# First FFN layer as seven block products with a running sum in PSUM, its operands streamed like the last layer's, and the h2 sums, the residual and the weight sums on GpSimd

## The chip, the cores and the metric

One core of one Trainium2 chip runs the whole program. The metric is the device time of one execution in microseconds (us); lower is better.

## What is computed

Cut to what matters (16 graphs of 1024 nodes, 256 features, 8 experts; everything in fp32):

```python
x = x + gnn(layernorm(x), adj, W, a)              # attention over the graph, per graph 1024 x 1024
n = layernorm(x)                                  # from here on: the FFN layer
w = softmax(mean(n, axis=0) @ Wr + br)            # 8 gates per node
h = relu(bn1(einsum('bfd,edh->bfeh', n, W1) + b1))    # first layer, 8 experts
h = relu(bn2(einsum('bfeh,ehk->bfek', h, W2) + b2))   # second layer
y = einsum('bfeh,ehd->bfed', h, Wo) + bo              # last layer
x = x + einsum('bfed,fe->bfd', y, w)
```

## The kernel before, in words

`attention_block` goes through the 16 graphs in 8 pairs of 16 row tiles (128 rows each) and writes x1, the input of the FFN, to HBM. Beside it each pair loads two matrices of W1 and W2 and splits them into an upper and a lower fp32r part (ACT L742, POOL L539); they stay in SBUF. Its last slots also start the FFN: normalisation of tile 0, the first gates, the first matmuls of step 0.

`ffn_block` works on 32 tiles of 512 rows (kept transposed: 2 blocks of 128 features by 512 rows) and, for each, on 8 experts: 256 steps. Every product is made in three matmuls (upper x upper, upper x lower, lower x upper), so each operand is first split: ACT copies it to fp32r (the upper part), DVE subtracts that from the original (the lower part). One step is:

- first layer (`z_layer(0, ...)`, L53 to L55): 2 x 2 blocks, 12 matmuls of 512 columns, into two PSUM banks; ACT applies batch norm and relu (L1331), splits (L1361), DVE makes the lower part (L1446);
- second layer (`z_layer(1, ...)`): again 12 matmuls of 512 columns; ACT batch norm and relu (L1331);
- DVE multiplies by the gate (L1488) and makes the block sums T1, T3 (L1495), T2 (L1498), T4 (L1501) of the seven-product scheme (Strassen's, in Winograd's form); ACT splits 7 blocks of 256 columns at once (L1347), DVE makes their lower part (L1481);
- last layer (`y_layer`, L1199 to L1202): seven block products, 21 matmuls of 256 columns, summed over the 8 experts in PSUM. Its weight sums are made in the first 8 steps by DVE and ACT (`LastWeights`), stored to HBM, and from step 8 on 896 KB of operands are loaded per step (L1105), beside 256 KB of gate rows (L1082).

The order of the work is written out by hand. Each engine runs `slot(u)` for u = -4 to 255 in its own instruction order; slot u holds the last layer of step u, the second layer of step u+2 and the first layer of step u+4. Engines meet only through semaphores, and each runs its list strictly in order. Work that comes once per tile (8 slots) is put into named slots: transposes of x (L1172) and y (L1180) on PE, copies of the seven sums out of PSUM (ACT L1386, DVE L1510), their combination (L1430), the lower part of x (L1409), the residual (L1422) and layer-norm statistics (L74, L81) on DVE, normalisation (L1315) on ACT. GpSimd has only five operations of 4 columns per tile (L87 to L90, L1148 to L1155).

Of the kernel before, what the change touches and what calls it, by code (L numbers as in the profile page):

```python
# [23 lines left out]
ALU = mybir.AluOpType  # L24
# [33 lines left out]
class TileNorm:  # L58
# [3 lines left out]
    def __init__(self, keep, sem, minus_half, ln_eps, CT, D):  # L62
        self.CT, self.minus_half, self.ln_eps = CT, minus_half, ln_eps
        self.xn = keep("ffn_xn", [P, CT, D])
        self.stats, self.mv = keep("ffn_stats", [P, CT, 6]), keep("ffn_mv", [P, CT, 2])
        self.vareps, self.rstd = keep("ffn_vareps", [P, CT]), keep("ffn_rstd", [P, CT])
        self.stat, self.mv_ready, self.vareps_ready = sem("ffn_stat"), sem("ffn_mv_ready"), sem("ffn_vareps_ready")
        self.rstd_ready, self.xn_ready = sem("ffn_rstd_ready"), sem("ffn_xn_ready")

    def statistics(self, dve, x1, x1_in, turn, rows=None):  # L70

        dve.wait_ge(x1_in, DMA * turn)
        for s in range(self.CT) if rows is None else rows:
            dve.bn_stats(self.stats[:, s, :], x1[:, s, :]).then_inc(self.stat, 1)  # L74

    def mean_var(self, dve, n, waited):

        if not waited:
            dve.wait_ge(self.stat, self.CT * n)
        for s in range(self.CT):  # L80
            last = dve.bn_aggr(self.mv[:, s, :], self.stats[:, s, :])  # L81
        last.then_inc(self.mv_ready, 1)

    def deviation(self, pool, n):

        pool.wait_ge(self.mv_ready, n)
        pool.tensor_tensor(self.vareps[:, :], self.mv[:, :, 1], self.ln_eps[:, :], ALU.add) \  # L87
            .then_inc(self.vareps_ready, 1)
        pool.wait_ge(self.vareps_ready, n)
        pool.tensor_tensor(self.rstd[:, :], self.vareps[:, :], self.minus_half[:, :], ALU.pow) \  # L90
            .then_inc(self.rstd_ready, 1)

    def normalise(self, dve, x1, n):

        dve.wait_ge(self.rstd_ready, n)
        for s in range(self.CT):
            last = dve.tensor_scalar(self.xn[:, s, :], x1[:, s, :], self.mv[:, s, 0:1], self.rstd[:, s:s + 1],
                                     ALU.subtract, ALU.mult)
        last.then_inc(self.xn_ready, 1)


class FirstTile:
# [15 lines left out]
class LastWeights:
# [5 lines left out]
    def __init__(self, sem, shared, Wo):  # L124
        self.Wo, self.E, self.KB = Wo, Wo.shape[0], Wo.shape[1] // P
        self.ops = [shared.wh_lo[:, 0:7, :].rearrange("p q (h c) -> p (q h) c", h=2)
                    .rearrange("p (i q) c -> p i q c", i=2), None]
        self.sums = [shared.x_rows[:, i * 4:(i + 1) * 4, :].rearrange("p s (h d) -> p (s h) d", d=P) for i in range(2)]
        self.loaded = [sem(f"wo_sums_in{i}") for i in range(4)]
        self.sum_ready, self.hi_ready, self.lo_ready = sem("wo_sum_ready"), sem("wo_hi_ready"), sem("wo_lo_ready")  # L130

    def home(self, e):

        return (0, 0) if e == 0 else ((1, 2, 3)[(e - 1) % 3], (e - 1) // 3)

    def load(self, sp, e):
        i, _ = self.home(e)
        for m in range(self.KB):
            sp.dma_start(self.sums[i][:, (1 - m):4:2, :],
                         self.Wo[e].rearrange("(k p) d -> p k d", p=P)[:, :, m * P:(m + 1) * P]) \  # L140
                .then_inc(self.loaded[i], DMA)

    def add_blocks(self, dve, e):

        i, turn = self.home(e)
        s, done = self.sums[i], 4 * e
        dve.wait_ge(self.loaded[i], DMA * self.KB * (turn + 1))
# [86 lines left out]
def program(nc, x, adj, W, a, Wr, br, W1, b1, g1, be1, m1, v1, W2, b2, g2, be2, m2, v2, Wo, bo, out):  # L234
# [1341 lines left out]
```

## Time and profile before

| | |
|---|---|
| median of 3 runs | 2841.0 us (2841.0 to 2842.17) |
| the profiled execution, its own time | 2841.68 us |
| its span, first to last instruction | 2839.8 us |
| busy: PE, PE weight loads, DVE, ACT, POOL | 2779.0, 2472.5, 2403.8, 2116.8, 487.6 us |
| attention, then FFN (first FFN instruction) | about 708.7 us, then 2131 us |
| DMA moved | 445.91 MB, mean 157 GB/s |

Matmul records overlap (each lasts longer than the distance to the next), so the distance between starts is what one costs PE. "idle before" is the engine's idle time ahead of an instruction with what ended it; "issue" there means that nothing the profile shows was waited for. Times in timelines are us from the start of the span.

### The profile page before, as it was taken

How to read it: one execution, taken by the hardware profiler on the slowest of the kernel's cores; microseconds unless marked ns; L12 is line 12 of the kernel's file. 1: busy time of each engine (PE TensorE's matmuls, PEld its weight loads, DVE VectorE, ACT ScalarE, POOL GpSimd, SP SyncE). 2: the span in 40 equal slices, each digit the busy share in tenths (PEclk: the TensorE clock that was granted, in tenths of full speed). 3: DMA queues.
4: the chain of work that ended last, by engine and by line, in shares of the span. 5: the costliest groups of instructions: out<-in, count | busy, mean ns of one | idle time of the engine just before them, and what ended most of it. 6: DMA issues, size and time to landing. Idle time of an engine off the chain costs nothing.

```text
span 2839.8 us, 46078 instructions
## 1 busy us (share of the span) xinstructions
PE 2779.0 (98%) x17110; PEld 2472.5 (87%) x17110; DVE 2403.8 (85%) x3376; ACT 2116.8 (75%) x2847; POOL 487.6 (17%) x704
## 2 busy tenths in 40 slices
PE   7999999998899999999999999999999999999998
PEld 7999999998788888888888888888888888888887
DVE  7999999997788888888888888888888888888887
ACT  6888888887677777767777767777777777777775
POOL 3555555455000000000000001000000000000000
PEclk9999999999999999999999999999999999999999
DMA  4555455443454554555545544555555555545454
GB/s 146 162 159 161 151 163 160 153 158 98 132 170 151 170 158 157 167 158 161 165 153 161 164 153 162 159 164 164 153 168 165 153 162 165 155 159 165 151 163 141
DMA packets 160060, 445.91 MB, mean 157 GB/s; under 512 B 16032, under 2 KB 73800, under 8 KB 159840
## 3 DMA queue, kind: packets, MB, share of 16 engines
q1 hardware_dynamic: 159840, 442.98, 49.7%
q8 instruction: 138, 2.26, 0.3%
q14 instruction: 82, 0.67, 0.1%
HBM read 401.99 MB, written 40.93 MB: 156 GB/s over the span
## 4 chain that ended last, share of the span: by engine, by line
PE 73%; DVE 1%; ACT 0%; issue 0%; DMA 0%; POOL 0%; DVEq 0%; ACTq 0%; POOLq 0%
PE head_ps L53 12%; PE head_ps L55 12%; PE head_ps L54 12%; PE m_ps L1199 7%; PE m_ps L1201 7%; PE m_ps L1202 7%; PE z_ps L53 4%; PE z_ps L55 4%; PE z_ps L54 4%; PE turn_ps L1172 1%; PE turn_ps L1180 1%; ACT h L1331 0%; DVE h_sums L1488 0%; DVE h_lo L1446 0%; DMA wo_ops<-wo_scratch 0%
## 5 line engine op out<-in xcount | busy, mean ns | idle before, releaser
L1331 ACT ACTIVATE h<-head_ps,bn_shift,bn_scale 128x512 f32<-128x512 f32 x768 | 593.7, 773 | 538.8 <-PE head_ps L55 331.7
L1481 DVE TENSOR_TENSOR h_lo<-h_sums,h_hi 128x1792 fp32r<-128x1792 f32 (+1 forms) x257 | 518.3, 2017 | 198.9 <-ACT h_hi L1347 198.8
L1347 ACT ACTIVATE h_hi<-h_sums 128x1792 fp32r<-128x1792 f32 (+1 forms) x257 | 435.5, 1694 | 63.3 <-DVE h_sums L1501 57.9
L1488 DVE TENSOR_TENSOR h_sums<-h,gate_row 128x1024 f32<-128x1024 f32 x256 | 313.8, 1226 | 121.0 <-ACT h L1331 103.7
L87 POOL TENSOR_TENSOR ffn_vareps<-ffn_mv,ln_eps 128x4 f32<-128x4 f32 x32 | 7.9, 248 | 1865.7 <-DVE ffn_mv L81 1865.7
L1446 DVE TENSOR_TENSOR h_lo<-h,h_hi 128x1024 fp32r<-128x1024 f32 x256 | 312.0, 1219 | 6.9 <-ACT h_hi L1361 6.9
L53 PE MATMUL attn_ps<-wh_hi,pT_hi 128*128 128x256 f32 x1024 | 305.1, 298 | 0.0
L54 PE MATMUL attn_ps<-wh_lo,pT_hi 128*128 128x256 f32 x1024 | 288.4, 282 | 0.0
L55 PE MATMUL attn_ps<-wh_hi,pT_lo 128*128 128x256 f32 x1024 | 288.4, 282 | 0.0
L1361 ACT ACTIVATE h_hi<-h 128x1024 fp32r<-128x1024 f32 x256 | 270.8, 1058 | 0.1
L1199 PE MATMUL m_ps<-h_hi,wo_ops 128*128 128x256 f32 x896 | 256.6, 286 | 3.0 <-DMA wo_ops<-wo_scratch 3.0
L1199 PE MATMUL m_ps<-h_hi,wh_lo 128*128 128x256 f32 x896 | 256.3, 286 | 0.0
L1201 PE MATMUL m_ps<-h_lo,wo_ops 128*128 128x256 f32 x896 | 250.8, 280 | 0.0
L1201 PE MATMUL m_ps<-h_lo,wh_lo 128*128 128x256 f32 x896 | 250.4, 279 | 0.0
L1202 PE MATMUL m_ps<-h_hi,wo_ops 128*128 128x256 f32 x896 | 250.3, 279 | 0.0
L1202 PE MATMUL m_ps<-h_hi,wh_lo 128*128 128x256 f32 x896 | 250.1, 279 | 0.0
L53 PE MATMUL head_ps<-wh_hi,w_hi 128*128 128x512 f32 x512 | 204.4, 399 | 7.4 <-ACT h L1331 7.4
L55 PE MATMUL head_ps<-wh_hi,w_lo 128*128 128x512 f32 x512 | 203.2, 397 | 0.0
L54 PE MATMUL head_ps<-wh_hi,w_hi 128*128 128x512 f32 x512 | 203.2, 397 | 0.0
L53 PE MATMUL head_ps<-xT_hi,w_hi 128*128 128x512 f32 x512 | 202.7, 396 | 0.0
L55 PE MATMUL head_ps<-h_hi,w_lo 128*128 128x512 f32 x512 | 201.3, 393 | 0.0
L53 PE MATMUL z_ps<-h_hi,w_hi 128*128 128x512 f32 x512 | 200.7, 392 | 0.5 <-DVE h_lo L1446 0.4
(198 smaller groups left out, 7619.1 us busy)
## 6 DMA issues: line engine op xcount, KB each, us to landing
wh_lo<-wo_scratch SPq DMA_DIRECT2D x124, 896.0 KB, 6.3
wo_ops<-wo_scratch SPq DMA_DIRECT2D x124, 896.0 KB, 6.5
adj_sb<-in_adj SPq DMA_DIRECT2D x128, 512.0 KB, 3.5
gate_row<-w_scratch SPq DMA_DIRECT2D x256, 256.0 KB, 4.6
x_sb<-in_x SPq DMA_DIRECT2D x64, 256.0 KB, 2.9
x_scratch<-x_sb SPq DMA_DIRECT2D x128, 128.0 KB, 1.9
ffn_x<-x_scratch SPq DMA_DIRECT2D x16, 512.0 KB, 7.6
x_sb<-x_scratch SPq DMA_DIRECT2D x16, 512.0 KB, 7.7
```

The source lines that it names most:

```text
L53: pe.matmul(out, w_hi, x_hi, start=first, stop=False)
L54: pe.matmul(out, w_hi, x_lo, start=False, stop=False)
L55: return pe.matmul(out, w_lo, x_hi, start=False, stop=last)
L1199: pe.matmul(m_at(q), w_hi, x_hi[:, x, :], start=e == 0 and q in OPENERS, stop=False, skip_group_check=True)
L1201: pe.matmul(m_at(q), w_hi, x_lo[:, x, :], start=False, stop=False, skip_group_check=True)
L1202: done = pe.matmul(m_at(q), w_lo, x_hi[:, x, :], start=False, stop=e == E - 1, skip_group_check=True)
L1331: return act.activation(dst, src, ACT.Relu, bias=bn_shift[layer][:, col], scale=bn_scale[layer][:, col])
L1347: act.activation(h2_hi[s % 2][:, a:b, :], g2[:, 1 + a:1 + b, :], ACT.Copy) \
L1361: act.activation(h1_hi[s % 2][:, :, :], h1[:, :, :], ACT.Copy).then_inc(S["h1_hi_ready"], 1)
L1446: dve.tensor_tensor(h1_lo[s % 2][:, :, :], h1[:, :, :], bits(h1_hi[s % 2][:, :, :]), ALU.subtract) \
L1481: dve.tensor_tensor(h2_lo[s % 2][:, a:b, :], g2[:, 1 + a:1 + b, :], bits(h2_hi[s % 2][:, a:b, :]), ALU.subtract).then_inc(S["h2_lo_ready"], 1)
L1488: dve.tensor_tensor(h2_rows, h2[:, :, :], gate[s % 2][:, :].unsqueeze(1).to_broadcast([P, KB, BANK]), ALU.mult).then_inc(S["gated_ready"], 1)
```

## The change

The first layer is made by seven block products too. The order of the work on PE in slot u (z = u+4, s2 = u+2) is now written as pieces between which ACT reads the running sum:

```diff
+            def extend_run(s, a, t, done):
+                pe.wait_ge(S["snap_ready"], 3 * s + done)
+                first_product(s, run, a, t, False, done == 3).then_inc(S["run_psum"], 1)
+            def corners(s):
+                wait(pe, S["c12_ready"], s)
+                first_product(s, Z_P2, A12, B21, True, True)
+                first_product(s, Z_P5, S1, T1, False, False).then_inc(S["c_psum"], 1)
...
             def slot(u):
+                second_layer(u + 2, 0)      # 6 matmuls of 512 columns
+                last_corner(z - 1)          # 3 of 256: S4 x B22
+                begin_run(z)                # 3: A11 x B11
...
+                last_layer(u, 0, 2)         # 6 of 256
+                second_layer(s2, 1)         # 6 of 512; waits relu2_ready
+                extend_run(z, S2, T2, 1)    # 3
+                corners(z)                  # 6
+                last_layer(u, 2, 4)         # 6
+                extend_run(z, S3, T3, 2)    # 3
+                last_layer(u, 4, 6)         # 6
+                extend_run(z, A22, T4, 3)   # 3
+                last_layer(u, 6, 7)         # 3
```

(The calls are written shorter than in the file; there each stands behind `is_step`.) ACT takes three snapshots of the running sum (256 columns, with the batch-norm shift) and the final value; the batch-norm scale is multiplied into W1 beforehand. DVE adds the corners, and its split now applies relu as well:

```diff
+            def snapshot(s, i):
+                act.wait_ge(S["run_psum"], 4 * s + (i + 1))
+                dst = (snaps[:, 0, :], h1_flat[:, 0:HALF], snaps[:, 1, :])[i]
+                act.activation(dst, run, ACT.Identity, bias=bn_shift[0][:, at:at + 1]).then_inc(S["snap_ready"], 1)
+            def first_sums(s):
+                dve.tensor_tensor(h1_flat[:, HALF:3 * HALF], snaps[...], bank_c, ALU.add)
+            def last_sum_first(s):
+                dve.tensor_tensor(h1_flat[:, 0:HALF], h1_flat[:, 0:HALF], Z_P5, ALU.add)
+            def first_lower(s, part):         # 256 and 768 columns, both operands in SBUF
+                dve.scalar_tensor_tensor(h1_lo, h1_flat, 0.0, bits(h1_hi), ALU.max, ALU.subtract)
```

Order in ACT's slot: `first_upper(z-1, 1)` (768 columns), `second_relu(s2, 0)`, `snapshot(z, 0)`, `first_upper(z-1, 0)` (256), `second_upper(s2-1, 1)` (1024), per-tile copies, `second_relu(s2, 1)`, `snapshot(z, 1)`, `blocks.upper(t, 1)` (1024, one slot in 8), `normalise`, `snapshot(z, 2)`, `second_upper(s2, 0)` (768), `c21(z)`, and in one slot in 8 the copy of the products. Order in DVE's slot: `second_lower(s2-1, 0)` (768), `first_lower(z-1, 1)` (768), `last_sum_first`, combinations, `blocks.lower` (768, 1024), `first_lower(z-1, 0)` (256), `second_lower(s2-1, 1)` (1024), `add_out`, `gated` (1024), `first_sums` (512), product copy.

The block sums of h2 move from DVE to GpSimd, with the residual and new block sums of x:

```diff
         def _(pool):
+            def residual(t, half):            # 512 columns, twice per tile
+                pool.tensor_tensor(rows, rows, w_bo[...], ALU.add)
+            def sums(s):                      # 512, 256, 256 columns
+                pool.wait_ge(S["gated_ready"], s + 1)
+                wait(pool, S["h2_lo1_ready"], s)
+                pool.tensor_tensor(g2[:, T1:T1 + 2, :], g2[:, B12, :]..., g2[:, B11:B11 + 2, :], ALU.subtract)
+                pool.tensor_tensor(g2[:, T2, :], g2[:, B22, :], g2[:, T1, :], ALU.subtract)
+                pool.tensor_tensor(g2[:, T4, :], g2[:, B21, :], g2[:, T2, :], ALU.subtract)
             def slot(u):
+                t = rows_due(u - 1, 1)        # u mod 8 == 2
+                if t is not None:
+                    blocks.sums(pool, t)      # 512, 256, 256 columns; waits for ACT's copies
+                for half in range(2):         # u mod 8 == 3 and 4
+                    residual(...)
+                sums(u + Z2)
```

The sums of W1 (scaled) and Wo, their split and their store move into the attention, on GpSimd (`OperandPrep`): per pair two scalings of 256 columns, eight sums of 128, two copies of 896 and two subtractions each of 384 and 512 columns; one of two weight splits (ACT L742, POOL L539) goes. In the FFN, SP loads 896 KB of W1 operands per step beside the 896 KB of Wo operands, the former after `c12_psum` of two steps before. Statistics of x1 are no longer made in the FFN: the mean and deviation that the attention computed are kept. The first matmuls of step 0 move from the attention's end into the FFN's first slot. The second layer's two halves now share one PSUM bank.

## Rows read from the trace of the kernel before

**Rows 1.** Engines' busy time over two stretches, attention and FFN.
```profile
core 0: us, PE busy (x) PEld busy (x) DVE busy (x) ACT busy (x) POOL busy (x), PEclk, DMA share, GB/s
100.00:700.00 600.00, 577.97 (x4476) 552.63 (x4475) 546.71 (x1016) 524.79 (x951) 329.97 (x474) 1.00 0.48 153
800.00:2800.00 2000.00, 1999.93 (x11442) 1743.13 (x11441) 1675.03 (x2030) 1437.52 (x1673) 104.93 (x145) 1.00 0.52 161
```
**Rows 2.** Timeline of PE: first matmul of three layers in one step (start, us).
```profile
2627.09 0.28 PE L1199 MATMUL m_ps<-h_hi,wo_ops 128*128 128x256 f32 x1
...
2629.54 0.39 PE L53 MATMUL head_ps<-xT_hi,w_hi 128*128 128x512 f32 x1
...
2632.29 0.39 PE L53 MATMUL z_ps<-h_hi,w_hi 128*128 128x512 f32 x1
```
**Rows 3.** Timeline of SP: the same issue one tile (8 steps) apart.
```profile
1529.83 0.32 SPq L1082 DMA_DIRECT2D gate_row<-w_scratch  x1
...
1595.59 0.32 SPq L1082 DMA_DIRECT2D gate_row<-w_scratch  x1
```
**Rows 4.** Groups of ACT and DVE, 1000 to 2700 us: busy, mean ns | idle before.
```profile
L1331 ACT ACTIVATE h<-head_ps,bn_shift,bn_scale 128x512 f32<-128x512 f32 x621 | 480.1, 773 | 432.8 <-PE head_ps L55 254.1 <-DVE h_lo L1446 178.6
L1481 DVE TENSOR_TENSOR h_lo<-h_sums,h_hi 128x1792 fp32r<-128x1792 f32 x208 | 421.1, 2025 | 164.0 <-ACT h_hi L1347 164.0
L1361 ACT ACTIVATE h_hi<-h 128x1024 fp32r<-128x1024 f32 x207 | 219.0, 1058 | 0.0
L1488 DVE TENSOR_TENSOR h_sums<-h,gate_row 128x1024 f32<-128x1024 f32 x207 | 253.7, 1226 | 94.4 <-ACT h L1331 80.2 <-DVE h_lo L1481 0.5
L1495 DVE TENSOR_TENSOR h_sums<-h_sums 128x512 f32<-128x512 f32 x207 | 141.7, 684 | 0.0
L1498 DVE TENSOR_TENSOR h_sums<-h_sums 128x256 f32<-128x256 f32 x207 | 88.0, 425 | 7.2
```
**Rows 5.** Groups of ACT in the attention: an evacuation of 256 columns with one column operand.
```profile
L728 ACT ACTIVATE wh_hi<-head_ps,xs_rstd 128x256 fp32r<-128x256 f32 x124 | 51.9, 470 | 2.4 <-PE head_ps L628 2.4
```
**Rows 6.** Timeline: PE to ACT, and PE starting again behind ACT.
```profile
1501.47 0.39 PE L55 MATMUL head_ps<-h_hi,w_lo 128*128 128x512 f32 x1
...
1501.91 0.78 ACT L1331 ACTIVATE h<-head_ps,bn_shift,bn_scale 128x512 f32<-128x512 f32 x1 [0.32 <-PE head_ps L55]
...
734.94 0.78 ACT L1331 ACTIVATE h<-head_ps,bn_shift,bn_scale 128x512 f32<-128x512 f32 x1
...
735.78 0.50 PE L53 MATMUL head_ps<-wh_hi,w_hi 128*128 128x512 f32 x1 [1.16 <-ACT h L1331]
...
736.12 0.40 PE L54 MATMUL head_ps<-wh_hi,w_hi 128*128 128x512 f32 x1
```
**Rows 7.** Groups of POOL, whole run.
```profile
L533 POOL TENSOR_TENSOR node_table<-node_table,n_sb 128x512 f32<-128x512 f32 x65 | 84.1, 1294 | 5.1
...
L522 POOL TENSOR_TENSOR xs_vareps<-xs_mv,ln_eps 128x2 f32<-128x2 f32 x64 | 12.5, 195 | 42.4 <-DVE xs_mv L857 42.4
```
**Rows 8.** Timelines of POOL and DVE in the attention, three meetings.
```profile
351.02 1.27 POOL L533 TENSOR_TENSOR node_table<-node_table,n_sb 128x512 f32<-128x512 f32 x1
352.26 1.10 POOL L562 TENSOR_SCALAR n_sb<-x_sb,x_negmean,x_rstd 128x256 f32<-128x256 f32 x2
...
352.94 1.50 DVE L905 SCALAR_TENSOR_TENSOR scores<-adj_sb,ej_rows 128x1024 f32<-128x1024 int32 x1 [1.07 <-issue]
...
329.66 1.20 DVE L905 SCALAR_TENSOR_TENSOR scores<-adj_sb,ej_rows 128x1024 f32<-128x1024 int32 x1
...
329.78 1.66 POOL L525 TENSOR_TENSOR xs_rstd<-xs_vareps,minus_half 128x2 f32<-128x2 f32 x1
...
332.51 0.69 POOL L525 TENSOR_TENSOR xs_rstd<-xs_vareps,minus_half 128x2 f32<-128x2 f32 x1
...
298.53 2.06 POOL L562 TENSOR_SCALAR n_sb<-x_sb,x_negmean,x_rstd 128x256 f32<-128x256 f32 x2
...
299.89 1.23 DVE L913 TENSOR_TENSOR pT_lo<-pT_ps,pT_hi 128x1024 fp32r<-128x1024 f32 x1 [0.26 <-ACT pT_hi L760]
```
**Rows 9.** Timeline of PE: the longest wait at the FFN's start.
```profile
748.72 0.80 PE L53 MATMUL head_ps<-wh_hi,w_hi 128*128 128x512 f32 x1 [4.66 <-ACT h L1331]
749.32 0.63 PE L54 MATMUL head_ps<-wh_hi,w_hi 128*128 128x512 f32 x1
749.75 0.63 PE L55 MATMUL head_ps<-wh_hi,w_lo 128*128 128x512 f32 x1
```
**Rows 10.** DMA issues, whole run: KB each, median us from issue to landing.
```profile
wo_ops<-wo_scratch SPq DMA_DIRECT2D x124, 896.0 KB, 6.5
...
gate_row<-w_scratch SPq DMA_DIRECT2D x256, 256.0 KB, 4.6
```

More of the change, by code:

```diff
@@ L84, in deviation @@
[L84 to L98, printed above, removed]
-        last.then_inc(self.xn_ready, 1)
+        self.negmean, self.rstd, self.shift = (keep(f"row_{n}", [P, tiles]) for n in ("negmean", "rstd", "shift"))
@@ L113, in __init__ @@
         self.wT = norm.xn[:, 0:2, :].rearrange("p s d -> p (s d)")
         self.wh_lo = keep("wh_lo0", [P, TB, D], FP32R)
+        self.wo_ops = self.wh_lo[:, 0:7, :].rearrange("p q (h c) -> p (q h) c", h=2).rearrange("p (i q) c -> p i q c", i=2)
+        self.w1_ops = keep("w1_ops0", [P, 2, 7, P], FP32R)
+        self.wo_in, self.w1_in = sem("wo_ops_in0"), sem("w1_ops_in0")
         self.x_rows = keep("x_sb0", [P, TB, D])
-class LastWeights:
+class OperandPrep:
     A21, A11, A22, A12, S1, S3, S2, S4 = range(8)
[L124 to L137, printed above, removed]
-        for m in range(self.KB):
[L139 to L147, printed above, removed]
@@ new lines, in scale_blocks, with sums @@
+    def scale_blocks(self, pool, e):
+        pool.wait_ge(self.blocks_in, 2 * DMA * (2 * e + 1))
+        pool.wait_ge(self.scale_in, DMA * (e + 1))
+        for m in range(self.KB):
+            part = self.blocks[:, (1 - m):4:2, :]
+            pool.tensor_tensor(part, part,
+                               self.scale[:, m * P:(m + 1) * P].unsqueeze(1).to_broadcast([P, self.KB, P]), ALU.mult) \
+                .then_inc(self.scaled, 1)
+    def sums(self, pool, n):
+        b, done = self.blocks, 4 * n
+        if n % 2 == 0:
+            pool.wait_ge(self.scaled, n + 2)
+        else:
+            pool.wait_ge(self.blocks_in, 2 * DMA * (n + 1))
@@ L495, in _ @@
             sp.wait_ge(small_in, DMA * 13)
+            sp.wait_ge(prep.stored, DMA * 2 * E)
         @block.gpsimd
@@ L804, in slot @@
                     for d in range(KB):
[L805 to L807 removed]
+                        blocks.copy(act, head_ps[:, d, :], 0, d, norm.root)
                 if last and u == GATE_SLOT + 1:
[L809 removed]
+                    for part in range(2):
+                        blocks.upper(act, 0, part)
                 if last and u == GATE_SLOT + 2:
@@ L1129, in _ @@
             load_x1(1)
-            for e in range(2, 4):
-                last_w.load(sp, e)
+            load_wo(1)
             for u in range(-Z1, NS):
@@ new lines, in first_product, with begin_run @@
+            def first_product(s, acc, a, t, first, stop):
+                i = (s // E) % 2
+                return product(acc, w1_ops[s % 2], blocks.hi[i], blocks.lo[i], a, t, first, stop)
+            def begin_run(s):
+                pe.wait_ge(w1_in[s % 2], DMA * (s // 2 + 1))
+                if s % E == 0:
+                    pe.wait_ge(blocks.lo_ready, 2 * (s // E + 1))
+                wait(pe, S["c21_ready"], s)
+                first_product(s, run, A11, B11, True, False).then_inc(S["run_psum"], 1)
```

765 lines of the change are left out of this document (407 added, 358 removed).

## The prediction, made before the changed kernel was run

> **What bounds the kernel now.** First the busy times of two stretches [rows 1]: in the FFN, 74% of the span, PE is busy 1999.93 of 2000 us at a granted clock of 1.00, DVE 84%, ACT 72%, GpSimd 5%. Busy matmul records overlap, so next the distance between starts [rows 2]: 21 matmuls of 256 columns take 2.45 us (0.117 each) and 12 of 512 columns 2.75 us (0.229). One step is 2.45 + 2.75 + 2.75 = 7.95 us; 16 transposes per tile add about 1.8 us, so a tile should take 65.4 us, and SP's issues one tile apart show 65.76 [rows 3]. PE streams with no hole: only fewer columns on PE, or a hole, can change the FFN's time. Both can happen here. Other engines' waits [rows 4] are long (ACT 433 us for relu alone, 621 times) and cost nothing now; they are the cover that the change spends.
>
> **A. Columns on PE.** The first layer goes from 12 matmuls of 512 to 21 of 256 columns: 2.75 - 2.45 = 0.30 us by these rows; the tile's measured excess (65.76 against 65.4) puts some first layers a little higher, at most 0.34. I take 0.32 x 256 steps = **-82 us** (-77 to -87).
>
> **B. The running sum.** PE may add the next product to the running sum only after ACT has read it. Behind the last matmul of such a group ACT starts 0.44 us after that matmul's start, of which 0.23 is its own pace [rows 6]: 0.21 us late. The snapshot, 256 columns out of PSUM with one column operand, is priced by ACT's like evacuation, 0.47 us [rows 5]; PE starts 0.06 us after ACT's end, and its first matmul then costs 0.11 more than the pace (0.34 against 0.23) [rows 6]. Round trip: 0.21 + 0.47 + 0.06 + 0.11 = 0.85 us. Between first and second extension lie 12 matmuls (1.40 us), enough; between second and third 6, 0.70 us, not enough, even with ACT idle. That is 0.15 us per step; laid out against the other pieces I take 0.13 x 256 = **+33 us** (+20 to +60).
>
> **C. Once per tile, without GpSimd.** ACT's per-step work is 8 instructions besides relu; relu 0.66 start to start twice, splits of 768, 256, 1024 and 768 columns (0.85, 0.45, 1.0 and 0.75, scaled from 1058 ns for 1024 [rows 4]) and four PSUM reads of 0.37: 5.9 us of 7.8. In the slot of the product copy (about 0.95 on ACT, 0.87 on DVE, behind the last product) ACT starts the next slot late, its snapshots and splits slip, and PE waits 0.65 us: x 31 = **+20 us** (0 to +35).
>
> **D. Start and attention.** The weight sums leave the first 8 FFN steps, where PE once waited 4.66 us and then ran its 512 columns at 0.43 us, the 1.2 GHz level [rows 9]: -7. The ramp gets one first layer more and three round trips per step with nothing to cover them: +8. In the attention GpSimd gets some 10 us of work per pair of 84 us (by 1.29 us for 512 columns and 0.2 for the start [rows 7]); DVE's one op per tile with both inputs in SBUF can meet it, 16 ops at 12% and half a microsecond: +8, 0 to +25. Sum **+10 us**. SP's new waits and loads stand behind GpSimd work several slots old. Dropping one split per pair saves nothing, as ACT is idle 12% there. The statistics leave DVE (1.9 us per tile), which only helps C.
>
> **E. GpSimd and DVE share a way into SBUF.** This decides. Where both run, the trace shows [rows 8]: DVE's 1024-column op with both inputs in SBUF was ready at 351.87, behind GpSimd's 351.02 and 352.26; it is recorded from 352.94 and lasts 1.50 instead of 1.20, so it began at about 353.24, 1.37 us late and 0.12 before GpSimd's record ends (353.36). The other way round, GpSimd's 2-column op took 1.66 instead of 0.69 us and ended 0.58 after DVE's. With one input in PSUM DVE was not held (299.89, 1.23 us). So the two exclude each other, op by op.
>
> New on GpSimd per step: 512 + 256 + 256 columns, 1.29 + 0.74 + 0.74 (between 0.195 for 2 and 1.294 for 512 columns [rows 7]) + 0.2 for waits = 3.0 us. DVE's ops with both inputs in SBUF: 768 + 768 + 256 + 1024 + 1024 columns, 4.4 us start to start (1226 ns for 1024 [rows 4]). Together 7.4, in a step of 7.8, and 1.0 us of DVE's PSUM ops can lie beside GpSimd: a plain step still fits. Steps with tile work don't:
> - slot 2 of 8, where GpSimd makes the sums of the next x. Counted from the slot's start, the h2 sums of the slot before end at 2.1, the x sums (1.29 + 0.74 + 0.74 + waits) at 5.1, if DVE never stands in front. ACT's split of them (1.0) stands in its queue before the third snapshot, which PE needs by 6.8; so they must be ready at 5.2. In that stretch DVE has three subtractions of 768 columns (0.87 each), one after each of GpSimd's ops: 5.1 + 2.6 = 7.7, PE waits 2.4 us.
> - slots 3 and 4: 1.29 us of residual each ahead of the h2 sums, with the subtraction of 1024 columns for x and `add_out` on DVE: 7.4 + 1.3 + 1.1 = 9.8 against 8.2; half of the excess lies beside PSUM ops or in slack: 0.8 each.
> Sum 4.0 us per tile x 31 = **+124 us**. Bounds: 0, if the order happens to be kind, to +200, if GpSimd's chain also waits behind two DVE ops in a row (a further 1.3 to 1.5 us in slot 2, and 1 us more over slots 3 and 4).
>
> The Trainium skill (SBUF - State Buffer, section "SBUF: two separate sides") says that whichever of the two starts first keeps the shared ports for its whole instruction. By that, DVE would be held 0.12 us longer behind each of the some five meetings per tile, and the sum would be about 19 us more; the row above shows the release before the record's end, and the sum goes by the row.
>
> **Sum.** -82 + 33 + 20 + 10 + 124 = +105. The profiled execution took 2841.68 us (span 2839.8), 0.7 above the median: 2947 us.
>
> **What is hidden.** W1's operands double the loads: 2.23 MB instead of 1.31 per step. At 0.52 busy for 161 GB/s [rows 1] that is 0.93 busy at 7.8 us, still under 1; a W1 load is issued some 1.9 us into a slot, takes 6.5 us [rows 10] and is needed 9.5 into it: 1 us of cover, more in longer steps. Cost 0.
>
> **Rivals.**
> 1. *GpSimd's work slips between (faster).* A, B, C and D alone: -19, 2823 us; with every term at its good end 2790. For it: plain steps fit, and GpSimd was idle 95% of the FFN. Against: [rows 8], the exclusion recurs with each graph in the attention. It decides if the x sums are ready by 5.2 us of slot 2. Chance of faster 0.25, of no change 0.05.
> 2. *The forecast*, 2947, its own range 2900 to 2985. Chance 0.45.
> 3. *GpSimd starves (much slower).* DVE's ops in a row keep the interface; the x sums end after 9 us: 124 becomes 200, 3023 us; if waits of 4 us per tile also lower the clock as after the 4.66 us wait [rows 9], a few tens of us more. Chance 0.18.
> 4. *DMA becomes the bound.* 161 GB/s at 0.52 busy is 310 GB/s at most; if two streams reached only 245, a step would average 9.1 us against the 8.22 of now [rows 3]: +225, 3076 us with the 10 of D. Against: 0.93 busy by the present rate. Chance 0.07.
>
> **Numbers.** A measurement of this kernel tells 0.2%, some 6 us. Faster 0.25, same 0.05, slower 0.70. The range 2795 to 3020 leaves out the best end of 1 and the upper part of 3 and 4.
>
> **What would show it.** In the new profile: first-layer matmuls 0.117 apart; in a plain step one PE wait of 0.1 to 0.2 us ahead of the third extension, released by ACT's snapshot (B). Steps of 7.8 us with longer ones in slots 0 and 1 (C) and slot 2 near 10 us (E), where ACT idles ahead of the x split, released by GpSimd; GpSimd's 256-column ops recorded at up to 1.5 us instead of 0.74, DVE's with idle time "issue". The forecast is wrong if slot 2 is as short as the others, if a plain step exceeds 8 us (then an engine's order bounds it all along), or if PE waits on DMA.

## The result, and the profile after

| | before | after |
|---|---|---|
| median | 2841.0 us (4 runs, 2840.89 to 2842.17) | 2976.0 us (4 runs, 2975.08 to 2978.34) |
| ratio, 95% interval | | 1.0475 [1.0457, 1.0494] |
| span of the profiled execution | 2839.8 us | 2974.8 us |
| first load of the FFN issued by SP | 708.6 us | 733.9 us |
| one tile, mean of 27 | 65.70 us | 69.03 us |
| DMA moved | 445.91 MB | 697.09 MB |

The change makes the kernel 135 us slower; 2947 was forecast. Of the spans' difference 25 us lie in the attention, 110 in the FFN, and of these 90 in the 27 tiles (3.33 each).

Busy time over the two stretches of [rows 1], in the changed kernel:

```profile
100.00:700.00 600.00, 563.30 (x4318) 536.53 (x4318) 535.42 (x978) 509.88 (x919) 388.37 (x555) 1.00 0.55 176
800.00:2800.00 2000.00, 1931.41 (x12939) 1761.70 (x12937) 1719.64 (x1874) 1572.65 (x2571) 1103.87 (x837) 0.99 0.77 258
```

PE fell from 1999.93 to 1931.41 us busy of 2000: its stream of matmuls has holes now. GpSimd went from 105 to 1104 us. DMA's share rose from 0.52 to 0.77. Two issues of SP one tile apart, as in [rows 3], are 68.94 us apart instead of 65.76:

```profile
1523.08 0.32 SPq L1140 DMA_DIRECT2D gate_row<-w_scratch  x1
...
1592.02 0.32 SPq L1140 DMA_DIRECT2D gate_row<-w_scratch  x1
```

The waits in the steady part, 1000 to 2700 us (24.6 tiles; columns: engine, line, what it waited for, us in total, times, longest):

```profile
PE head_ps L1258 <- ACT z_snaps L1431: 44.6, 25, 1.8
DVE h L1558 <- issue: 41.0, 111, 0.7
...
ACT wh_hi L129 <- POOL xT_blocks L120: 22.5, 13, 1.7
...
ACT xT_hi L129 <- POOL xT_blocks L120: 20.5, 12, 1.7
...
PE head_ps L1258 <- DMA w_ops<-w_scratch: 4.1, 11, 0.7
```

Read it backwards: PE waits for a snapshot once per tile (25 times, 44.6 us), and ahead of it ACT has waited for GpSimd's sums of x (13 + 12 times, 43.0 us). That is the chain named for slot 2. The timelines of one such slot show it. First GpSimd:

```profile
1617.60 1.29 POOL L1217 TENSOR_TENSOR h_sums<-h_sums 128x512 f32<-128x512 f32 x1 [4.62 <-DVE h_sums L1586]
1618.97 1.33 POOL L1220 TENSOR_TENSOR h_sums<-h_sums 128x256 f32<-128x256 f32 x1
1620.38 1.33 POOL L1222 TENSOR_TENSOR h_sums<-h_sums 128x256 f32<-128x256 f32 x1
1621.68 2.01 POOL L115 TENSOR_TENSOR xT_blocks<-xT_blocks 128x512 f32<-128x512 f32 x1
1623.77 0.81 POOL L118 TENSOR_TENSOR xT_blocks<-xT_blocks 128x256 f32<-128x256 f32 x1
1624.66 1.60 POOL L120 TENSOR_TENSOR xT_blocks<-xT_blocks 128x256 f32<-128x256 f32 x1
```

then DVE, ACT and PE:

```profile
1621.38 1.16 DVE L135 TENSOR_TENSOR xT_lo<-xT_blocks,xT_hi 128x768 fp32r<-128x768 f32 x1
1622.46 1.51 DVE L1570 SCALAR_TENSOR_TENSOR h_lo<-h,h_hi 128x256 fp32r<-128x256 f32 x1
1623.89 1.77 DVE L1577 TENSOR_TENSOR h_lo<-h_sums,h_hi 128x1024 fp32r<-128x1024 f32 x1
```

```profile
1626.29 1.06 ACT L129 ACTIVATE xT_hi<-xT_blocks 128x1024 fp32r<-128x1024 f32 x1 [1.52 <-POOL xT_blocks L120]
1627.25 0.46 ACT L1431 ACTIVATE z_snaps<-head_ps,bn_shift 128x256 f32<-128x256 f32 x1
```

```profile
1626.15 0.28 PE L1260 MATMUL m_ps<-h_hi,wh_lo 128*128 128x256 f32 x1
1627.76 0.39 PE L1258 MATMUL head_ps<-wh_hi,w_ops 128*128 128x256 f32 x1 [1.33 <-ACT z_snaps L1431]
```

The two engines stretch each other's records in turn (a record is one line of the profile, start and duration). GpSimd's 512 columns take 2.01 instead of 1.30 us, since they began only behind DVE's 768; DVE's 256 columns, 0.42 us by themselves, are recorded with 1.51, since they ran behind GpSimd. In numbers: DVE's record ends at 1623.97, so it ran from 1623.55, which is 0.14 us before GpSimd's record ends (1623.69); in [rows 8] it was 0.12. It is the same all along: in the 65 such records of 256 columns from 1000 to 2700 us that are stretched, DVE's work, counted back from its end, begins 0.13 or 0.14 us before a record of GpSimd ends, and GpSimd's stretched operations begin 0.12 to 0.15 us before one of DVE's ends. The Trainium skill (SBUF — State Buffer, section "SBUF: two separate sides") says that whoever starts first keeps the shared ports for the whole instruction. By the records' ends that would be 0 and isn't seen; but two operations of DVE in a row overlap by 0.08 us too (1621.38 + 1.16 against 1622.46), so a record may end later than its work, and these rows can't tell which it is. The chain in front of ACT's split is 8.7 us long (1617.60 to 1626.26). PE's first matmul of this slot began at 1618.62, so the x sums were ready 7.6 us into it (7.7 in the forecast), and PE stands for 1.5 us (2.0 in most tiles, where no load of W1 has held it before).

A wait of this kind has a second cost, which the TensorE clock shows. After the one of 1.82 us at 1558.56 the granted clock falls to 0.50, the 1.2 GHz level (the second row's columns are those of [rows 1]):

```profile
1558.56 0.39 PE L1258 MATMUL head_ps<-xT_hi,w_ops 128*128 128x256 f32 x1 [1.82 <-ACT z_snaps L1431]
```

```profile
1560.00:1562.00 2.00, 2.00 (x7) 1.61 (x6) 1.41 (x2) 0.71 (x2) 1.92 (x2) 0.50 0.77 234
```

Matmuls of 512 columns start 0.43 us apart there instead of 0.23. From 1000 to 2750 us this happens 11 times, each time right behind this wait and for some 3.4 us. It never happens there in the kernel before, nor with either kind of fill or with the sums of x on DVE (experiments 1, 2 and 4). Most of it is hidden, since slot 3 waits for DVE and GpSimd anyway: the ten whole tiles that have it take 69.24 us, the fifteen others 68.89, so it costs some 4 of the 110 us.

### The profile page after: what moved, and what is told of

Its sections match the earlier page's. It is cut to its first block, busy times and chain, and to the rows that moved or that the text cites. A ratio compares the mean times of both kernels' runs of the same rounds, so it can differ in the third digit from the quotient of the medians.

```text
span 2974.8 us, 54565 instructions
## 1 busy us (share of the span) xinstructions
PE 2819.2 (95%) x19414; PEld 2594.3 (87%) x19414; DVE 2536.7 (85%) x3271; ACT 2338.2 (79%) x3918; POOL 1682.4 (57%) x1597
## 2 busy tenths in 40 slices
DMA packets 204669, 697.09 MB, mean 234 GB/s; under 512 B 22704, under 2 KB 83544, under 8 KB 204400
## 4 chain that ended last, share of the span: by engine, by line
PE 40%; POOL 9%; ACT 8%; DVE 8%; DMA 4%; issue 4%; ACTq 0%; DVEq 0%; POOLq 0%
PE head_ps L1258 6%; PE z_ps L55 4%; PE z_ps L53 4%; PE z_ps L54 4%; PE head_ps L1260 4%; PE head_ps L1259 4%; PE m_ps L1258 4%; PE m_ps L1259 4%; PE m_ps L1260 4%; DMA w_ops<-w_scratch 4%; ACT h_hi L1469 3%; DVE h_lo L1570 3%; POOL xT_blocks L115 2%; DVE h_sums L1586 2%; ACT h L1457 2%
## 5 line engine op out<-in xcount | busy, mean ns | idle before, releaser
L1217 POOL TENSOR_TENSOR h_sums<-h_sums 128x512 f32<-128x512 f32 x256 | 332.1, 1297 | 964.6 <-DVE h_sums L1586 964.6
L1577 DVE TENSOR_TENSOR h_lo<-h_sums,h_hi 128x768 fp32r<-128x768 f32 (+1 forms) x512 | 633.1, 1236 | 74.7 <-ACT h_hi L1469 74.2
L1570 DVE SCALAR_TENSOR_TENSOR h_lo<-h,h_hi 128x768 fp32r<-128x768 f32 (+1 forms) x512 | 501.0, 979 | 111.6 <-ACT h_hi L1449 105.2
L1469 ACT ACTIVATE h_hi<-h_sums 128x768 fp32r<-128x768 f32 (+1 forms) x512 | 482.7, 943 | 46.2 <-DVE h_sums L1586 40.1
L1259 PE MATMUL head_ps<-xT_lo,w_ops 128*128 128x256 f32 x1792 | 506.9, 283 | 0.0
L1457 ACT ACTIVATE h<-z_ps,bn_shift,bn_scale 128x512 f32<-128x512 f32 x512 | 397.3, 776 | 132.0 <-PE z_ps L55 129.0
L55 PE MATMUL z_ps<-h_hi,w_lo 128*128 128x512 f32 x1024 | 409.0, 399 | 0.0
L54 PE MATMUL z_ps<-h_lo,w_hi 128*128 128x512 f32 x1024 | 408.8, 399 | 0.0
L1259 PEld LDWEIGHTS head_ps<-xT_lo,w_ops 128*128 128x128 f32 x1792 | 342.0, 191 | 22.9
L1222 POOL TENSOR_TENSOR h_sums<-h_sums 128x256 f32<-128x256 f32 x256 | 328.4, 1283 | 20.1
L1220 POOL TENSOR_TENSOR h_sums<-h_sums 128x256 f32<-128x256 f32 x256 | 323.8, 1265 | 20.1
L53 PE MATMUL attn_ps<-wh_hi,pT_hi 128*128 128x256 f32 x1024 | 306.3, 299 | 0.0
```

What stands on the lines that cost most here:

```text
L53: pe.matmul(out, w_hi, x_hi, start=first, stop=False)
L54: pe.matmul(out, w_hi, x_lo, start=False, stop=False)
L55: return pe.matmul(out, w_lo, x_hi, start=False, stop=last)
L1217: pool.tensor_tensor(g2[:, T1:T1 + 2, :], g2[:, B12, :].unsqueeze(1).to_broadcast([P, 2, HALF]), g2[:, B11:B11 + 2, :], ALU.subtract).then ...
L1222: pool.tensor_tensor(g2[:, T4, :], g2[:, B21, :], g2[:, T2, :], ALU.subtract).then_inc(S["t4_ready"], 1)
L1259: pe.matmul(acc, w_hi, x_lo[:, t - 1, :], start=False, stop=False, skip_group_check=True)
```

## The experiments

**How a slot is measured.** ACT reads the final value of the running sum once per step. The mean distance between two such starts, by slot of the tile, over 24 to 27 tiles from 1000 to 2750 us (each row is a run below, by its number; "fills" are memsets in place of GpSimd's arithmetic):

| slot | 0 | 1 | 2 | 3 | 4 | 5 | 6 | 7 | tile |
|---|---|---|---|---|---|---|---|---|---|
| changed kernel | 8.72 | 8.79 | 9.99 | 9.47 | 8.50 | 7.78 | 7.84 | 7.93 | 69.02 |
| 1, long fills | 8.38 | 8.57 | 8.03 | 8.34 | 8.30 | 7.87 | 7.86 | 7.91 | 65.26 |
| 2, short fills | 8.38 | 8.57 | 7.92 | 8.31 | 8.32 | 7.89 | 7.86 | 7.94 | 65.18 |
| 8, short fills, more cover | 8.61 | 8.72 | 7.78 | 8.21 | 8.18 | 7.75 | 7.78 | 7.79 | 64.83 |
| 3, h2 sums on DVE | 9.12 | 9.41 | 10.60 | 8.72 | 8.58 | 7.99 | 8.14 | 8.14 | 70.71 |
| 4, x sums on DVE | 8.80 | 8.78 | 8.99 | 9.59 | 8.61 | 7.74 | 7.79 | 7.90 | 68.20 |
| 7, W1 loaded once | 8.70 | 8.81 | 9.96 | 9.47 | 8.50 | 7.78 | 7.80 | 7.87 | 68.92 |
| 11, copies | 8.60 | 8.73 | 9.83 | 9.21 | 8.41 | 7.61 | 7.85 | 7.97 | 68.20 |

(Slots 0, 1, 3 and 4 hold four transposes each, some 0.44 us.)

**1 and 2. Take the reads away, keep the time.** GpSimd's arithmetic in the FFN becomes memsets, which write but read nothing:

```diff
-pool.tensor_tensor(g2[:, T1:T1 + 2, :], g2[:, B12, :]..., g2[:, B11:B11 + 2, :], ALU.subtract)
+fill(pool, g2[:, T1:T1 + 4, :], S["t13_ready"], 1024, 4)   # 4 memsets of 256 columns
...
-pool.tensor_tensor(rows, rows, w_bo[:, at:at + CT // 2, :], ALU.add)
+fill(pool, rows, S["residual_ready"], 512, 12)
```

> In the FFN, GpSimd's sums of h2, its sums of x and the residual are replaced by memsets that take about as long as the records of the changed kernel show (1.30, 1.26, 1.29; 2.0, 0.8, 1.6; 1.6 us), but read nothing; the products are not the reference's. Theory (GpSimd and a DVE operation with both inputs in SBUF exclude each other): DVE is no longer held, slot 2 stays long because its chain on GpSimd stays 4.7 us long, the others go back to 7.8 to 8.6: a tile of 66.7 us instead of 69.1, about 2890 us (2870 to 2910). Rival (GpSimd is only slow, its own durations in the chain are the loss): nothing changes, 2970 to 2980.

> The same with memsets as long as GpSimd's operations are when nothing stands against them (1.25, 0.74, 0.74; residual 1.25 us). Theory (exclusion): what the forecast had without its part E, 64.6 us per tile, about 2830 us (2815 to 2850), below the kernel before. Rival (GpSimd's own durations, no exclusion): only the chain in slot 2 gets shorter, by 1.7 us per tile, about 2920 us. If memsets hold the interface as well: nothing changes.

Measured: 2861.27 us (2855.99 to 2864.68), ratio to before 1.0069 [1.0054, 1.0085], and 2854.0 us (2851.72 to 2859.27), 1.0048 [1.0033, 1.0063]. The first lies just below the 2870 to 2910 expected, the second just above its 2815 to 2850, and both far from the rivals. So 115 and 122 us of the change's loss go with GpSimd's reads of SBUF. (The fills' data are wrong, but that gives PE no faster clock than before: the kernel before is granted 1.00 in this stretch too.) DVE's groups, 1000 to 2700 us, in the changed kernel:

```profile
L1570 DVE SCALAR_TENSOR_TENSOR h_lo<-h,h_hi 128x768 fp32r<-128x768 f32 x198 | 242.9, 1227 | 31.7 <-ACT h_hi L1449 26.6
...
L1570 DVE SCALAR_TENSOR_TENSOR h_lo<-h,h_hi 128x256 fp32r<-128x256 f32 x197 | 149.0, 756 | 48.6 <-ACT h_hi L1449 48.6
L1558 DVE TENSOR_TENSOR h<-z_snaps,head_ps 128x512 f32<-128x512 f32 x197 | 135.1, 686 | 59.0 <-issue 41.0 <-ACT z_snaps L1431 16.8
```

and the same three with short fills:

```profile
L1578 DVE SCALAR_TENSOR_TENSOR h_lo<-h,h_hi 128x768 fp32r<-128x768 f32 x209 | 200.3, 958 | 78.1 <-ACT h_hi L1457 78.0
...
L1566 DVE TENSOR_TENSOR h<-z_snaps,head_ps 128x512 f32<-128x512 f32 x208 | 143.1, 688 | 105.9 <-ACT z_snaps L1439 73.0 <-issue 32.9
L1578 DVE SCALAR_TENSOR_TENSOR h_lo<-h,h_hi 128x256 fp32r<-128x256 f32 x209 | 88.4, 423 | 59.8 <-ACT h_hi L1457 59.8
```

With both inputs in SBUF, 756 ns become 423 and 1227 become 958. With one input in PSUM (the sum of 512 columns) it is 686 against 688: not held. The Trainium skill (SBUF — State Buffer, section "SBUF: two separate sides") says the same of a DVE operation with two SBUF inputs, "only against a GpSimd op that reads SBUF"; the memsets bear it out.

The long fills were meant to be as long as the held operations and came out shorter, 3.34 us per step against some 4.1 (1617.60 to 1621.71 above), and 3.44 for the x sums against 4.6. GpSimd's timeline with long fills:

```profile
1507.73 3.34 POOL L97 MEMSET h_sums<- 128x256 f32 x12 [5.18 <-DVE h_sums L1594]
1511.01 3.44 POOL L97 MEMSET xT_blocks<- 128x93 f32 x20
```

So they don't fully part "DVE is held" from "GpSimd's held operations get longer". Both are one exclusion; what falls is the rival that GpSimd's own durations are the loss, since the long fills are longer than its unheld operations. And the expectation that slot 2 stays long was wrong: 8.03 us. A chain of 3.3 + 3.4 us on GpSimd just fits there, one of 4.1 + 4.6 costs 2 us.

**3 and 4. Move sums back to DVE.** Once the three sums of h2, behind `first_sums`; once the three of x:

```diff
 def slot(u):                      # DVE, run 3
     first_sums(u + Z1)
+    sums(u + Z2)
...
     blocks.lower(dve, t, 0)       # DVE, run 4
+    blocks.sums(dve, t)
```

> Only the sums of h2 go back to DVE, behind first_sums. Theory: DVE gets 1.6 us of work per step for the 3 us of exclusion that it loses; laid out by hand 71.4 us per tile against 69.1, about +60 us, 3035 us (3000 to 3060). Rival (GpSimd's h2 sums are the loss as such, and DVE has room as 85% busy suggests): faster than the changed kernel, about 2880 us.

> Only the sums of x (three operations per tile) go to DVE, behind the first subtraction for x. Theory: the 4.4 us chain on GpSimd in slot 2 becomes 1.6 us on DVE; slot 2 falls from 9.95 to 8.5 us and slots 3 and 4 take a little back: -0.85 us per tile, about 2949 us (2930 to 2965). Rival (slot 2 is long because DVE is full there): no gain or a loss, 2975 to 3000.

Measured: 3031.68 us (3024.7 to 3037.56), ratio to before 1.067 [1.0649, 1.0691]; and 2951.14 us (2946.24 to 2954.71), 1.0392 [1.0374, 1.0409]. Both as the hand layout had it. Of the two places, GpSimd is the better one for the h2 sums even with the exclusion; for the x sums it isn't: slot 2 falls by 1.0 us, and only 0.3 come back in slots 0, 3 and 4. With the sums of x on DVE the granted clock no longer falls in the steady part either.

**5 and 6. The weight work in the attention,** once left out from the second pair on (semaphores counted up in its place), once replaced by memsets:

```diff
-if u == 0:
+if u == 0 and k == 0:
     prep.scale_blocks(pool, k)
+if u == 0 and k > 0:
+    pool.sem_inc(prep.scaled, 2)
```

> GpSimd's work on the weights in the attention (scalings, sums, copies, subtractions) is left out from the second pair on; its loads and stores and all semaphores stay; the products of seven experts are not the reference's. In the changed kernel the FFN begins 25 us later than in the kernel before, 17 of it spread over the pairs. Theory (this work on GpSimd makes the loss): the FFN begins about 715 us instead of 734, total 2976 - 17 to 22 = about 2956 us (2950 to 2962). Rival (the loss is from the wider layer-norm bookkeeping, the DMA traffic and the other order): 2970 to 2978 us.

> The same work replaced by memsets of about the same length (scalings 0.8, sums 0.5, copies 0.93, subtractions 1.15 us), which read nothing; the products are not the reference's. Theory A (exclusion with DVE's masked scores): as if the work were left out, about 2956 us. Theory B (GpSimd's list is in order, and its row denominators and deviations, for which DVE and PE wait, come late behind the weight work): no gain, 2970 to 2978 us. In between: both, by their shares.

Measured: 2971.02 us (2969.69 to 2975.43), ratio to before 1.0456 [1.044, 1.0471], and 2974.74 us (2971.02 to 2976.53), 1.0464 [1.0449, 1.048]. A miss: GpSimd's arithmetic is worth 5 us in all, not 17 to 22. Memsets give 1 us, as theory B had it, so the exclusion from SBUF is at most a small part of what this work costs in the attention.

The FFN's first load comes at 724.5 and 728.8 instead of 733.9 us (in kernels with an unchanged attention it varies from 728.4 to 734.6). From there to the gate load of step 34 run 5 takes 6.4 us longer, run 6 some 2. The granted clock shows what may eat the gain. Two stretches of 10 us, in the changed kernel and in run 5:

```profile
730.00:740.00 10.00, 5.51 (x23) 4.95 (x23) 1.23 (x1) 0.95 (x3) 4.26 (x7) 0.50 0.43 145
740.00:750.00 10.00, 7.26 (x45) 5.95 (x45) 4.05 (x6) 5.60 (x10) 0.00 (x0) 0.98 0.65 238
```

```profile
730.00:740.00 10.00, 8.30 (x30) 6.92 (x30) 3.09 (x5) 4.47 (x9) 0.00 (x0) 0.50 0.73 261
740.00:750.00 10.00, 10.00 (x39) 9.03 (x39) 2.04 (x4) 3.15 (x6) 0.00 (x0) 0.50 0.28 92
```

PE comes out of the idle stretches at the attention's end at the 1.2 GHz level in every form of the change. In the changed kernel that lasts some 13 us, in run 5 some 34. Over the runs a longer low stretch goes with slower first steps; nothing was changed to try it alone.

The waits of the changed kernel's attention, 60 to 680 us, name a cause of the loss:

```profile
PE head_ps L685 <- DVE wh_lo L931: 24.1, 21, 3.0
...
DVE xs_stats L914 <- DMA x_sb<-in_x: 15.1, 7, 3.7
...
DVE row_inv L942 <- POOL row_den L609: 8.2, 14, 0.6
```

Before, the second of these did not exist, the third was 0.2 us, and the first was

```profile
PE head_ps L614 <- DVE wh_lo L868: 5.2, 14, 0.4
```

So DVE is late, and PE waits 19 us more for it. Seven times, once per pair, rows of x are late. SP's timeline shows why:

```profile
208.88 0.33 SPq L485 DMA_DIRECT2D adj_sb<-in_adj  x1
209.25 0.43 SPq L224 DMA_DIRECT2D wo_scratch<-prep_ops  x1
209.73 0.43 SPq L503 DMA_DIRECT2D w_stage<-in_L_ffn_W  x1
210.21 2.81 SPq L175 DMA_DIRECT2D prep_blocks<-in_L_ffn_W  x2
213.06 0.54 SPq L180 DMA_DIRECT2D prep_scale<-scale_scratch  x1
213.64 0.47 SPq L511 DMA_DIRECT2D x_scratch<-x_sb  x1
214.16 0.43 SPq L481 DMA_DIRECT2D x_sb<-in_x  x1
```

Five DMAs, four of them new (`w_stage` was loaded in other slots before), take 4.4 us of SP's own time (the two loads of `prep_blocks` 1.4 each here) ahead of the load of x at 214.16, for which DVE stands until 219.02.

**7. W1's operands loaded once:**

```diff
-if 2 <= s < NS:
-    sp.wait_ge(S["c12_psum"], s - 1)
-    load_w1(s)
```

> The W1 operands are loaded for steps 0 and 1 alone and used for all steps; the products are not the reference's. In the changed kernel's steady part PE waits up to 0.5 us in slot 2 for such a load. Theory (these waits add to the others): -0.3 to -0.5 us per tile, 2961 to 2967 us. Rival (what PE does not wait there, it waits at the next snapshot, since GpSimd and DVE set the pace): 2972 to 2978 us.

Measured: 2975.85 us (2973.97 to 2977.36), ratio to before 1.0472 [1.0454, 1.0489]. The rival holds: slot 2 takes 9.96 instead of 9.99 us without any such wait. In the slot shown above PE's 0.35 us for W1 came 7 us ahead of its 1.33 us for the snapshot; without such waits those for the snapshots are longer in sum (45.5 instead of 44.6 us, and 8.5 instead of 6.3 for the second snapshot).

**8. More cover for the third snapshot,** in the kernel with short fills:

```diff
-last_layer(u, 4, 6)
+last_layer(u, 4, 7)
 extend_run(z, A22, T4, 3)
-last_layer(u, 6, 7)
```

> The kernel with short memsets (2854 us, without the exclusion), and in it the last three matmuls of the last layer are put ahead of the third extension of the running sum: 9 matmuls (1.05 us) instead of 6 (0.70) cover the third snapshot's round trip of 0.85. Theory (part B of the forecast, 0.13 us per step, is the uncovered round trip): it goes nearly whole, -33 us, 2821 us (2815 to 2832). Rival (the 0.13 is a price of coming back to the same sum, or the final value of the sum gets late instead): 2850 to 2860 us.

Measured: 2843.0 us (10 runs, 2837.72 to 2849.57), ratio to before 1.0004 [0.9994, 1.0013]; 11 us less than the 2854.0, and neither the 2815 to 2832 of the theory nor the 2850 to 2860 of its rival. In slots 2 to 7 the gain is 0.08 to 0.15 us each, 0.13 in the mean, so the round trip was rightly priced. But slots 0 and 1, behind the product copy, get 0.23 and 0.15 longer. Two rows of this run, 1000 to 2700 us, show how, first ACT's final read of the running sum, then PE:

```profile
L1444 ACT ACTIVATE h<-head_ps,bn_shift 128x256 f32<-128x256 f32 x210 | 99.9, 476 | 42.0 <-PE head_ps L1268 41.9
```

```profile
PE head_ps L1266 <- ACT h L1437: 7.2, 26, 0.6
```

ACT now waits 0.2 us for the last product before this read (0.0 with short fills alone), so the copy behind it is later, and PE waits for the second snapshot once per tile (0.2 us in all with short fills alone). That the later copy is the link between the two is argued from ACT's order, not tried. Also, the profiled execution is at the 1.2 GHz level for some 30 us at the FFN's start, the one with short fills alone for some 13, and the ten executions spread over 12 us. The working of the round trip can be read in the changed kernel itself, PE, then ACT, then PE:

```profile
1635.25 0.28 PE L1260 MATMUL head_ps<-wh_hi,w_ops 128*128 128x256 f32 x1
...
1635.96 0.28 PE L1260 MATMUL m_ps<-h_hi,wo_ops 128*128 128x256 f32 x1
1636.10 0.39 PE L1258 MATMUL head_ps<-wh_hi,w_ops 128*128 128x256 f32 x1
1636.33 0.28 PE L1259 MATMUL head_ps<-xT_lo,w_ops 128*128 128x256 f32 x1
```

```profile
1635.57 0.48 ACT L1431 ACTIVATE z_snaps<-head_ps,bn_shift 128x256 f32<-128x256 f32 x1 [0.95 <-PE head_ps L1260]
```

Last matmul of the second extension at 1635.25, snapshot 1635.57 to 1636.05, next extension at 1636.10; 0.02 us late, and its first matmul takes 0.23 instead of 0.12: 0.13 together.

**9, 10 and 12. SP's group behind the load of x.** Run 9 moves it from slot 13 to 14, and GpSimd's first weight work one slot with it; run 10 adds the x sums on DVE; run 12 is run 10 with GpSimd's work left where it was:

```diff
-if u == 13:                       # SP, runs 9, 10, 12
+if u == 14:
     prep.store(sp, 2 * k + 1)
...
-if u == 0:                        # GpSimd, runs 9 and 10
+if u == 1:
     prep.scale_blocks(pool, k)
```

> Only the order of SP in the attention changes: the store of weight operands and the loads behind it (five DMAs, 1.4 MB, some 4.4 us of SP's own time) go from slot 13, ahead of the load of the next rows of x, to slot 14, behind it; GpSimd's first weight work goes from slot 0 to slot 1. In the changed kernel DVE waits seven times, once per pair, for these rows, 15.1 us in all, and the weight work on GpSimd was worth only 5 us. Theory (this queue makes most of the attention's loss): these waits go, -10 to -15 us, 2961 to 2966 us. Rival (PE's stream is held by something else in the same slots, such as the DMA rate): within 4 us of 2976.

> The same, and the sums of x on DVE as in the run that took 2951 us. If the two gains are independent (one lies in the attention, one in the FFN): 2951 - 13 = 2938 us (2934 to 2944). Still slower than the kernel before by 3.4%.

> The sums of x on DVE, and in the attention only SP's group of five DMAs goes from slot 13 to slot 14; GpSimd's weight work stays in slot 0. In the run that moved both, DVE's seven waits for rows of x were gone, but GpSimd's weight work in slot 1, 3.5 us, stood between its normalisation and the next row denominators, and DVE waited 20.1 us for those (8.2 in the changed kernel). Theory (the two effects are separate): the waits for x go and the new ones do not come: 2951 - 8 to 13 = 2940 us (2936 to 2945). Rival (the loads, issued one slot later, arrive late for GpSimd in slot 0 and push the row denominators, or PE's time in the attention is held by the sum of DVE's and GpSimd's work): 2948 to 2962 us.

Measured: run 9 2986.65 us (2981.31 to 2989.54), ratio to before 1.0509 [1.0493, 1.0525], 11 us worse than the changed kernel, which neither the theory nor its rival had. Run 10 2959.59 us (2958.31 to 2962.2), 1.0418 [1.0401, 1.0436], 8 us worse than the x sums alone instead of 13 better. The wait for x is gone in run 9, and this one stands in its place:

```profile
DVE row_inv L942 <- POOL row_den L609: 20.1, 15, 3.2
```

GpSimd's slot 1 holds its normalisation, and the weight work now followed it and stood ahead of the next row denominators. In run 12 they don't meet; its DVE wait, 60 to 680 us:

```profile
DVE row_inv L942 <- POOL row_den L609: 9.5, 15, 1.4
```

The wait for rows of x is gone, and PE's for `wh_lo` is 13.4 us instead of 24.1. One pair of graphs (DVE's mask of the first tile to that of the next pair) takes, from the second pair on, 83.6 us before, 86.2 to 86.8 in the changed kernel (89.9 once), 87.4 in run 9 and 85.0 in run 12: about half of what a pair lost comes back.

Run 12: 2944.0 us (5 runs, 2938.43 to 2945.91), ratio to before 1.0357 [1.0343, 1.0371], against 1.0392 with the x sums alone; 7 us gained, 8 to 13 expected. The FFN's first load is at 722.2 us, 6 earlier than in run 4, but the clock is at the 1.2 GHz level from there to some 745 us. It is the fastest form of the change that computes all of it, and still 3.6% slower than the kernel before.

**11. Copies instead of memsets,** one input in SBUF:

```diff
-pool.tensor_tensor(g2[:, T2, :], g2[:, B22, :], g2[:, T1, :], ALU.subtract)
+pool.tensor_copy(g2[:, T1:T1 + 3, :], g2[:, B12:B12 + 3, :])     # 768 columns
```

> GpSimd's sums of h2 and x and the residual are replaced by copies with one input in SBUF (1024, 768 and 768 columns, about 1.05, 0.8 and 0.8 us by its copy of 896 columns in 929 ns; the residual's 512 columns 0.55 us); the products are not the reference's. Theory A (every operation of GpSimd that reads SBUF excludes DVE's with two inputs in SBUF): GpSimd's time that excludes is nearly the same in a plain step (2.65 instead of 2.78 us) and smaller in slots 2 to 4, so 2930 to 2960 us. Theory B (only operations with two inputs on both sides exclude): as with memsets, 2845 to 2865 us.

Measured: 2950.43 us (2947.86 to 2952.78), ratio to before 1.0384 [1.0368, 1.0399]. Theory A. GpSimd's groups, 1000 to 2700 us:

```profile
L1220 POOL COPY h_sums<-h_sums 128x768 f32<-128x768 f32 x199 | 274.0, 1377 | 12.3
L1218 POOL COPY h_sums<-h_sums 128x768 f32<-128x768 f32 x199 | 267.8, 1345 | 12.3
L1216 POOL COPY h_sums<-h_sums 128x1024 f32<-128x1024 f32 x199 | 207.6, 1043 | 761.4 <-DVE h_sums L1584 761.4
```

768 columns take longer than 1024: the first copy is not held, the two others are. One SBUF input on GpSimd's side is enough.

## Why the prediction was right

The time came out 29 us above the 2947, inside the likeliest case's own range, and the mechanism that was to decide decides: it is worth 119 of the 135 us. That the parts around it add up as well is in part luck, as the steps show:

- **A, columns on PE (-82).** In the kernel before, 24 matmuls of 512 columns in a row take 5.54 us (1545.09 to 1550.63), 12 of them 2.77; 21 of 256 take 21 x 0.118 = 2.48: -0.29 x 256 = -75. The 0.32 had added a remainder of the tile to the rows' own 0.30; that was wrong.
- **B, running sum (+33).** 0.13 us per step as predicted, read above; 33.
- **C, product copy (+20).** With short fills slots 0 and 1 exceed slots 3 and 4, which hold the same transposes, by 0.06 and 0.25 us, 10 us in all instead of 20. In the changed kernel slots 0 and 1 are 0.34 and 0.22 longer than that, within the exclusion's share.
- **E, exclusion (+124).** Tile 69.03 against 65.20 us with short fills: 3.8 x 31 = 119; by the medians 122. The places: +2.07 in slot 2 (2.4 predicted), +1.16 and +0.18 in slots 3 and 4 (0.8 each), and +0.34 and +0.22 in slots 0 and 1 (nothing predicted). The sum is better than its parts. In slot 2 itself two errors cancel: GpSimd's h2 sums end 3.1 us into it, not 2.1, and the sums of x take 4.6 us, not 5.6, which gives 7.6 against 7.7. PE then stands 1.5 us in the slot shown and 2.0 in most, not 2.4. That the waits would lower the clock, which only rival 3 had, does occur (0.2 us of slot 3's 1.16).
- **DMA (0).** Right in effect, wrong in its reason: the 1 us of cover for a W1 load isn't always there (PE waits 4.1 us for them in 1700), but the waits cost nothing beside the others (run 7). In the kernel with short fills undisturbed tiles take 64.94 us and the mean is 65.20; PE's idle time ahead of W1's loads there (2.6 us in 26 tiles) is 0.10 of the 0.26, the rest stays open.
- **D, attention (+8) and start (+1).** This step failed: +25 in the attention. The prediction said that "SP's new waits and loads stand behind GpSimd work several slots old". It looked at what SP waits for, not at what waits behind SP: its five issues take 4.4 us and stand ahead of a load of x. That was worth 7 us by run 12. GpSimd's arithmetic is worth 5 more (run 5), if the two add. About half of the 25 is not explained by a run; DVE's wait for row denominators rose from 0.2 to 8.2 us, and DMA's share from 0.48 to 0.55, and neither was taken away alone. From the FFN's first load to the gate load of step 34 it is 306.3 instead of 286.5 us, 20 more, of which some 13 are four tiles at 3.33; the rest, 7, is the ramp, the FFN's first steps. The prediction had +1 for it, and no term for the clock, which is at the 1.2 GHz level for some 13 us there.

Together: -75 + 33 + 10 + 119 + 25 + some 7 of ramp and 8 of disturbed tiles without the exclusion (0.26 x 31) = +127, of the 135 measured. The 8 left are not accounted for.

Of the rivals, the first (no exclusion, 2823) was run almost as such: 2854 with short fills, 2843 with more cover. The change's gain on PE is real but small, and even without the exclusion the attention's loss eats it. The third (GpSimd starves, 3023) did not come: the x sums were ready 7.6 us into slot 2, not 9. Nor did the fourth (DMA the bound, 3076): at 258 GB/s its busy share is 0.77, and loading W1 once changes nothing (run 7).

## What to carry to other kernels

Before moving work from DVE to GpSimd, write down for each step which DVE operations read two inputs from SBUF and how long GpSimd reads SBUF at all, and add them: the sum, not each engine's share, has to fit into the step, and into the fullest step of the tile. A busy share of 86% beside 55% (the window above) says nothing of it; the sign is one shape with two durations, as 423 and 756 ns here. And when DMAs are added to an in-order queue, ask which load stands behind them, and count the issue time beside the bytes. A wait of PE is to be priced with the clock that follows it: look at the granted clock behind each.

## What the runs showed of the hardware

- The holding is seen as a longer record, not as a wait: DVE's 256 columns take 423 ns free, 756 ns in the mean of the changed kernel and 1.52 us at worst, GpSimd's 256 columns 0.74 us at best and 1.33 us in most steps. A memset on GpSimd holds nothing; a copy with one input does.
- What a DMA costs SP to issue isn't fixed by its bytes. The 32 loads of `prep_blocks` (128 KB, runs of 128 columns) have records of 0.43 to 1.61 us, 22 of them over 1 us; the loads of 896 KB in the FFN 0.32 in the median.
- A wait of PE can lower its clock: behind 11 of 26 waits of 1.3 to 1.8 us from 1000 to 2750 us the granted clock was 0.50 for some 3.4 us. In runs 1, 2, 4 and 8, which lack these waits, it was 1.00 all through that stretch.
- PE's first matmul of 256 columns behind a wait costs 0.11 us more, whether the wait was 0.02 or 1.33 us (1627.76 to 1627.98 is 0.22 as well).
- Records of memsets in a row overlap: 12 of 256 columns, 312 ns each by their group's mean, take 3.34 us.
